# First cross attention of a gated cross-attention block: negative maxima added by TensorE in PSUM, rstd by a GpSimd power

## What is computed

```python
x = x + jnp.tanh(g_xattn[0]) * _L0_xattn_ref(_layernorm(x, axis=-1), ctx_1024, ...)
# inside, 16 sequences, 64 queries and 64 context rows (48 main, 16 "dca"), 16 heads of 16
q = _ln((x @ Wq + bq).reshape(b, s1, H, HD), qn_w, qn_b)
k = _ln(kv[..., :HD], kn_w, kn_b)
k_dca = _ln(kv_dca[:, :, 0], kn_dca_w, kn_dca_b)
ctx = _attn(qT, k..., v...)               # softmax(q k^T / 4) v over the 48 main rows
ctx_dca = _attn(qT, k_dca..., v_dca...)   # the same over the 16 dca rows, its own softmax
return (ctx + DCA_WEIGHT * ctx_dca) @ Wo + bo
# _ln divides by sqrt(var + 1e-6) within each head
```

## Time and profile before

| | |
|---|---|
| median of 3 runs | 534.36 us (534.05 to 830.44) |
| span of the profiled execution, first to last instruction | 530.4 us |
| median less span | 4.0 us |
| phase A in that span | up to about 161 us |
| busy in the span | PE 443.2, DVE 362.0, ACT 199.5, POOL 170.8 us |

### The profile page before, as it was taken

One profiled execution on the slowest core, in us unless ns is written; L12 is line 12 of the kernel. 1 busy time (PEld: TensorE's weight loads), 2 busy tenths in 40 slices (PEclk: granted clock), 3 DMA queues, 4 the chain that ended last, 5 costly groups with the idle time before them and its releaser, 6 DMA issues.

```text
span 530.4 us, 8960 instructions
## 1 busy us (share of the span) xinstructions
PE 443.2 (84%) x2992; PEld 399.9 (75%) x2992; DVE 362.0 (68%) x785; ACT 199.5 (38%) x390; POOL 170.8 (32%) x204
## 2 busy tenths in 40 slices
PE   0575948666468999999998999989999998989996
PEld 0455837555468889898997978968998896888886
DVE  5768688695506557585757698698788779855542
ACT  2355535363221333233233534454344344423331
POOL 3004132232300221212123453564454365333322
PEclk9958886959556999999899969998996998999999
DMA  8111010100200020010201001001000100000000
GB/s 242 30 59 59 1 59 0 60 2 6 93 1 0 1 99 0 15 83 0 99 0 53 1 0 53 1 0 51 0 0 1 50 0 0 0 0 21 20 20 21
DMA packets 6628, 15.96 MB, mean 30 GB/s; under 512 B 1090, under 2 KB 4291, under 8 KB 6100
## 3 DMA queue, kind: packets, MB, share of 16 engines
q1 hardware_dynamic: 6612, 15.75, 9.1%
HBM read 14.70 MB, written 1.05 MB: 30 GB/s over the span
## 4 chain that ended last, share of the span: by engine, by line
PE 51%; issue 17%; DVE 13%; POOL 11%; ACT 4%; DMA 3%; POOLq 0%; DVEq 0%; ACTq 0%; SPq 0%
PE ps L287 34%; DVE work L1277 4%; PE ps L1071 3%; PE ps L468 3%; POOL work L1329 2%; POOL workr L1453 2%; PE ps L803 2%; POOL workA L554 2%; PE ps L458 2%; PE ps L824 2%; PE ps L827 1%; POOL wB_lo L560 1%; PE ps L258 1%; DMA stage<-in_wC 1%; PE ps L1083 1%
## 5 line engine op out<-in xcount | busy, mean ns | idle before, releaser
L287 PE MATMUL ps<-xT_hi,wB_hi 128*128 128x256 f32 x224 | 67.7, 302 | 1.7 <-POOL wB_lo L1334 1.7
L287 PE MATMUL ps<-xT_lo,wB_hi 128*128 128x256 f32 x224 | 64.6, 289 | 0.0
L287 PE MATMUL ps<-xT_hi,wB_lo 128*128 128x256 f32 x224 | 64.4, 288 | 0.0
L287 PE MATMUL ps<-wB_hi,workr 128*128 128x256 f32 (+1 forms) x224 | 52.4, 297 | 3.8 <-POOL workr L1453 3.4
L287 PE MATMUL ps<-wN_hi,shared_r 128*128 128x256 f32 x256 | 52.7, 301 | 0.0
L995 POOL TENSOR_TENSOR workr<-work,workr 128x256 fp32r<-128x256 f32 (+1 forms) x36 | 22.9, 636 | 83.8 <-ACT workr L878 83.8
L287 PEld LDWEIGHTS ps<-xT_hi,wB_hi 128*128 128x128 f32 x224 | 44.1, 197 | 4.0 <-issue 1.9
L1329 POOL TENSOR_SCALAR work<-work,lut_step,lut 128x344 f32<-128x344 int32 (+1 forms) x72 | 46.5, 660 | 1.6 <-POOL wB_lo L1334 1.6
L1277 DVE COPY_PREDICATED work<-work 128x1376 f32<-128x1376 int32 (+5 forms) x36 | 43.6, 1212 | 4.0 <-DVE work L1277 1.1
L287 PEld LDWEIGHTS ps<-wN_hi,shared_r 128*128 128x128 f32 x256 | 43.9, 206 | 1.5 <-DVE shared_r L1240 1.5
L287 PEld LDWEIGHTS ps<-xT_lo,wB_hi 128*128 128x128 f32 x224 | 44.2, 197 | 0.0
(11 more groups left out here) (178 smaller groups left out, 1161.3 us busy)
## 6 DMA issues: line engine op xcount, KB each, us to landing
stage<-in_wC SPq DMA_DIRECT2D x4, 1280.0 KB, 5.4
stage<-in_wB SPq DMA_DIRECT2D x4, 768.0 KB, 4.3
stage<-in_idx SPq DMA_DIRECT2D x4, 536.0 KB, 4.0
stage<-in_wA SPq DMA_DIRECT2D x2, 512.0 KB, 5.6
out<-x SPq DMA_DIRECT2D x4, 256.0 KB, 2.2
x<-in_x SPq DMA_DIRECT2D x1, 768.0 KB, 7.2
ctx_T<-in_ctx_T SPq DMA_DIRECT2D x1, 512.0 KB, 7.6
ctx_n<-in_ctx_n SPq DMA_DIRECT2D x4, 128.0 KB, 2.2
```

The costliest lines, as they stand in the source:

```text
L287: last = nc.tensor.matmul(out, l, r, start=start and i == 0, stop=stop and i == 2)
```

## The change

1. VectorE writes the negated maxima of a tile as float32r (`dve_A_top`) and subtracts nothing. Both tiles' maxima stand at the head of the group.
2. TensorE adds them to the scores in PSUM: per tile four matmuls with the identity (a float32r copy, `ident_A`) as weights and the negated maxima, repeated 48 or 16 times, as the moving operand (`pe_A_shift`). The score matmuls leave their sums open for it. Both shifts stand behind the next group's query matmuls.
3. ScalarE's exponentials read PSUM and write `probs`; both stand before the next group's square.
4. ScalarE's logarithm and exponential of the variance and VectorE's three correcting instructions are gone; GpSimd raises the 128x64 variances to -0.5 (`pool_A_rstd`), behind the first tile's scaling, and in the start between the two layer-norm powers.

```diff
                     k = c * BG + 2 * t + b
                     last = nc.tensor.matmul(o[:, :, b, :], qx[:, k].rearrange("p h n -> p (h n)"),
-                                            kx[:, k], start=True, stop=True)
+                                            kx[:, k], start=b == 0, stop=False,
+                                            skip_group_check=True)
             last.then_inc(*A["scores_done"].up())
+
+        def pe_A_shift(pe, g, t):
+
+            pe.wait_ge(*A["maxed"].at(g, 2 * t + 2))
+            for c in range(2):
+                o = ps[:, 2 * t + c, :].rearrange("p (k n) -> p k n", n=S)
+                for i, (lo, hi) in enumerate(PARTS):
+                    first = 16 * i + 8 * c
+                    last = nc.tensor.matmul(o[:, :, lo:hi], ident_A, bc_last(neg_maxA[:, t, first:first + 8], hi - lo),
+                                            start=False, stop=True, skip_group_check=True)
+            last.then_inc(*A["shifted"].up())
...
-        def act_A_guess(act, n):
-
-            act.wait_ge(*A["grp_var"].at(n, 1))
-            nc.scalar.activation(gln, gvar, ACT.Ln).then_inc(*A["act"].up())
-            act.wait_ge(*A["act"].at(n, 1))
-            nc.scalar.activation(guess, gln, ACT.Exp, scale=-0.5).then_inc(*A["grp_guess"].up())
...
         def dve_A_scale(dve, n):
 
-            dve.wait_ge(*A["grp_guess"].at(n, 1))
-            nc.vector.tensor_tensor(gsq, guess, guess, ALU.mult).then_inc(*A["dve"].up())
-            dve.wait_ge(*A["dve"].at(n, 2))
-            nc.vector.scalar_tensor_tensor(out=gfix, in0=gsq, scalar=-0.5, in1=gvar, op0=ALU.mult,
-                                           op1=ALU.mult).then_inc(*A["dve"].up())
-            dve.wait_ge(*A["dve"].at(n, 3))
-            nc.vector.scalar_tensor_tensor(out=grs, in0=gfix, scalar=1.5, in1=guess, op0=ALU.add,
-                                           op1=ALU.mult).then_inc(*A["dve"].up())
-            dve.wait_ge(*A["dve"].at(n, 4))
+            dve.wait_ge(*A["grp_rstd"].at(n, 1))
             nc.vector.tensor_tensor(heads, heads, bc_last(grs, HD0), ALU.mult).then_inc(*A["scaled"].up())
...
         def act_A_exp(act, g, t):
-            act.wait_ge(*A["shifted"].at(g, 2 * t + 2))
-            v = split_tokens(probs[:, t])
-            nc.scalar.activation(v, v, ACT.Exp, scale=HD0 ** -0.5).then_inc(*A["exp_ready"].up())
+            act.wait_ge(*A["shifted"].at(g, t + 1))
+            nc.scalar.activation(split_tokens(probs[:, t]), split_tokens(ps[:, 2 * t:2 * t + 2, :]), ACT.Exp,
+                                 scale=HD0 ** -0.5).then_inc(*A["exp_ready"].up())
...
-        def dve_A_shift(dve, g, t):
+        def dve_A_top(dve, g, t):
 
             dve.wait_ge(*A["scores_done"].at(g, t + 1))
             s = split_tokens(ps[:, 2 * t:2 * t + 2, :]).rearrange("p (k n) -> p k n", n=S)
             for i, (lo, hi) in enumerate(PARTS):
-                nc.vector.tensor_reduce(mxA[:, t, 16 * i:16 * i + 16], s[:, :, lo:hi], AX,
-                                        ALU.max).then_inc(*A["maxed"].up())
-            for i, (lo, hi) in enumerate(PARTS):
-                dve.wait_ge(*A["maxed"].at(g, 2 * t + i + 1))
-                nc.vector.tensor_tensor(probs[:, t, :, lo:hi], s[:, :, lo:hi],
-                                        bc_last(mxA[:, t, 16 * i:16 * i + 16], hi - lo),
-                                        ALU.subtract).then_inc(*A["shifted"].up())
+                nc.vector.tensor_reduce(neg_maxA[:, t, 16 * i:16 * i + 16], s[:, :, lo:hi], AX,
+                                        ALU.max, negate=True).then_inc(*A["maxed"].up())
...
+            pe.wait_ge(ident_A_ready, 1)
 
         def pe_A(pe, g, more, two_more):
             n = g + 1
             if more:
                 pe_A_q(pe, n)
+            pe_A_shift(pe, g, 0)
+            pe_A_shift(pe, g, 1)
             pe_A_probs(pe, g, 0)
...
@@ -618,16 +617,13 @@
             n = g + 1
             act_A_prep(act, g)
             act_A_exp(act, g, 0)
+            act_A_exp(act, g, 1)
             if more:
                 act_A_square(act, n)
-                act_A_guess(act, n)
-            else:
-                act_A_exp(act, g, 1)
             if two_more:
                 act_A_ctx(act, g + 2)
             act_A_probs(act, g, 0)
             if more:
-                act_A_exp(act, g, 1)
                 act_A_qk(act, n)
                 act_A_k(act, n)
...
-            dve_A_shift(dve, g, 0)
+            dve_A_top(dve, g, 0)
+            dve_A_top(dve, g, 1)
             if more:
                 dve_A_kv(dve, n)
                 dve_A_q(dve, n)
             dve_A_sum(dve, g, 0)
             if more:
                 dve_A_var(dve, n)
-            dve_A_shift(dve, g, 1)
             if more:
                 front_stats(dve, g + 2, (g + 2) % GROUPS)
                 dve_A_scale(dve, n)
...
+        def pool_A_rstd(pool, n):
+
+            pool.wait_ge(*A["grp_var"].at(n, 1))
+            nc.gpsimd.tensor_tensor(grs, gvar, expo[:, 0:1].broadcast_to([P, 64]), ALU.pow
+                                    ).then_inc(*A["grp_rstd"].up())
+
         def pool_A_start(pool):
             front_pool(pool, 0)
+            pool_A_rstd(pool, 0)
             front_pool(pool, 1)
 
         def pool_A(pool, g, more, two_more):
+            n = g + 1
             pool_A_prep(pool, g)
             pool_A_scale(pool, g, 0)
             if more:
+                pool_A_rstd(pool, n)
                 front_pool(pool, g + 2)
             pool_A_scale(pool, g, 1)
```

More of the change, by code:

```diff
@@ L202, in build @@
         front = signals("front", stat=4, var_ready=1, rstd_ready=1, xn_ready=2, xT_done=1, hi_ready=1, lo_ready=1)
-        A = signals("A", dve=4, act=1, ctx_hi=2, ctx_lo=2, kv_done=2, q_done=1, kv_ready=6, q_ready=1,
-                    squared=1, grp_var=1, grp_guess=1, scaled=1, qT_done=2, kT_ready=2 * PAIRS0,
-                    qx_ready=2, scores_done=2, maxed=4, shifted=4, exp_ready=2, summed=4, recip_ready=2,
+        A = signals("A", dve=1, ctx_hi=2, ctx_lo=2, kv_done=2, q_done=1, kv_ready=6, q_ready=1,
+                    squared=1, grp_var=1, grp_rstd=1, scaled=1, qT_done=2, kT_ready=2 * PAIRS0,
+                    qx_ready=2, scores_done=2, maxed=4, shifted=2, exp_ready=2, summed=4, recip_ready=2,
                     probs_ready=4, pT_done=2, pT_ready=2, pv_done=1, an_ready=4, anT_done=1, an_hi=1, an_lo=1,
@@ L209, in build @@
         A_prep_in = sem("A_prep_in")
+        ident_A_ready = sem("ident_A_ready")
         CH = EC + 1
@@ L309, in build @@
         an = take(TILES * D).rearrange("p (t n) -> p t n", t=TILES)
-        gsum, gssq, gvar, gln, guess, gsq, gfix, grs = (take(64) for _ in range(8))
-        mxA, smA, rcA = (take(64).rearrange("p (t n) -> p t n", t=TILES) for _ in range(3))
+        gsum, gssq, gvar, grs = (take(64) for _ in range(4))
+        smA, rcA = (take(64).rearrange("p (t n) -> p t n", t=TILES) for _ in range(2))
         take_r = carver(workAr)
@@ L314, in build @@
         aT_hi, aT_lo = (take_r(DC * TG).rearrange("p (c n) -> p c n", c=DC) for _ in range(2))
+        neg_maxA = take_r(TILES * 32).rearrange("p (t n) -> p t n", t=TILES)
+        ident_A = take_r(P)
         def ctx_rows(g, lo, hi):
@@ L605, in act_A_start @@
             act_A_square(act, 0)
-            act_A_guess(act, 0)
+            act.wait_ge(const_in, 16)
+            nc.scalar.copy(ident_A, ident).then_inc(ident_A_ready, 1)
             front_upper(act, 1, 7)
```

2 lines of the change are left out of this document (1 added, 1 removed).

## The result

The changed kernel takes 569.81 us (median of 4 runs, 563.26 to 575.58) against 534.25 before: a ratio of 1.0587, 95% interval [1.0544, 1.063], so slower by some 6%.

What follows compares the result with a forecast made beforehand. Two almost level paths to TensorE's turn bound cross attention. Start +0.9, group 0 +1.1, waits -0.6 and group 3 -0.2 make +1.2 us; span 531.6 plus 4.0 gives 535.6 us, range 526 to 559.

Steps and rivals of the forecast that it cites:

- the power is long: Rival, GpSimd's queue between the two scalings: from X = 3.6 each us costs four; X = 8 gives 554 us; chance 0.27.
- the likeliest case: Power at 2.8 us, clock as before, shift at 0.52 us a tile: 535.6 us, the case alone spanning 532 to 545.
- X: Duration of GpSimd's 128x64 power to -0.5, in the start and groups 0 to 2: 2.8 us, bounds 0.83 and 20.2.
- 4X - 12.4: Change of the whole time in us once X exceeds 3.6, from the start and three groups; passes 2% at X = 5.8.
- start, X - 1.87: Head scaling in the start, queued behind the power: -0.7 us up to X = 1.15, X - 1.87 beyond, +0.9 at 2.8.
- groups 1 and 2, X - 3.6 - 0.2 each: Power free up to X = 3.6, one us per us beyond; the 0.2 us wait for GpSimd's second scaling is gained.
- group 0, the same, with the shift +1.1: Shift queued behind 12 key/value and 12 query matmuls, so the first tile's sums start later: +1.1 us.
- second path: VectorE's head scaling and second tile's sums, then GpSimd's second scaling: ends at 13.1 + X, T counted from the group's start.
- The first path: First tile's sums (T = 4.32), scaling, transposes, values and next group's turn, until T = 16.70; the change does not move it.
- The shift at full rate: TensorE's four shift matmuls per tile at 0.51 ns a column: 0.52 us, plus about 0.2 until ScalarE sees it.
- The rival of a float32 price: Shift matmuls on TensorE run as plain float32, 2.96 us a tile: 542.8 us, still within 2%; chance 0.06.
- Kept clock: Rival: shifts break TensorE's idle time, so it keeps full clock: 519.6 us, group 3 alone about 528; chance 0.09.

Runs made afterwards that it cites:

- power only: The kernel before with only GpSimd's 128x64 power in place of ScalarE's guess and VectorE's correction: 568.2 us, ratio 1.0639.
- long filling: The changed kernel with 30 unused identity transposes where TensorE waits for the scaled heads and 22 where it waits for the second scaling: 561.81 us, ratio 1.0534.
- shift only: The changed kernel without the power, ScalarE's guess and VectorE's correction put back in their old places: 533.81 us, ratio 1.0011.
- half-width run: The changed kernel with the power on 32 of the 64 columns, the others left at 1: 551.31 us, ratio 1.0342.
- old order: "shift only" with the kernel before's order in all three queues: 529.1 us, 0.9932; with 30 identity transposes ahead of the first tile's: 526.06 us, 0.9892.
- filled kernel before: The kernel before with 34 unused identity transposes after the query matmuls of each group: 539.96 us, ratio 1.0117.

## Why the prediction was wrong

I forecast 535.6 us, range 526 to 559, and gave "slower by over 2%" 0.27. Measured: 569.8, outside the range. The power makes the loss, as the rival "the power is long" has it; the likeliest case had the size of the power wrong.

**The step that failed is the term X**, the price of the 128x64 power, "the weakest number here". I had bounds of 0.83 and 20.2 us from rows, and both held: it is 10.52. My value of 2.8 came from an assumption that no row carried, that a power costs fifteen multiplies of 2.26 ns a column. It costs 0.158 us a column, 70 multiplies. Of the 0.63 us by which the two-column power exceeds a multiply's fixed part, half was in fact the columns' share (2 x 0.158). The upper bound, "all of it grows with the columns", was off by a factor of 2, my value by nearly 4. The figure for branches in the Trainium skill (GPSIMD Engine Reference, Performance versus the Vector engine), by which X was estimated at 1.3, was further off than mine: the trace has 10.52.

**The waits of the formula that turns X into time held; the clock was missing from it.** The rival "the power is long" gave 4X - 12.4, 2% from X = 5.8. With X = 10.52 that is +29.7, or 564.0 us; the two runs behind the ratio took 563.26 and 566.58, and 1.0587 times 534.25 is 565.6. How near that is owes something to luck, since the formula has no term for the clock behind the waits and even the groups of one execution differ in it. Its parts, read in "power only" and in the changed kernel with the long filling, where the clock was full behind the waits:

| term | forecast at X = 10.52 | power only | long filling |
|---|---|---|---|
| start, X - 1.87 | +8.65 | +8.2 | +8.1 |
| groups 1 and 2, X - 3.6 - 0.2 each | +6.7 | +7.3, +7.0 | +6.2, +6.0 |
| group 0, the same, with the shift +1.1 | +6.7 or +7.8 | +10.3, of it 3.4 half clock | +7.6 |

In the changed kernel itself the second path reads as forecast: the second scaling at T = 112.77 + 2.11 - 91.26 = 23.6, forecast 13.1 + X = 23.6.

**The first path.** "The first path does not move" was right: the sums of group 1 start at T = 95.58 - 91.26 = 4.32, forecast 4.32, and "shift only" measures 1.0011.

**The shift at full rate.** Right: four matmuls took 0.76 us with their pipeline, 0.52 plus 0.2 forecast. The rival of a float32 price (2.96) falls. With "shift only" group 0 is 0.6 us longer (1.1 forecast) and groups 1 and 2 are 0.3 and 0.4 us shorter (0.2 forecast). The row of 5.91 us behind the rival's price was not wholly at half clock (0.50 up to 37 us, 0.72 and 1.00 after it), so that price was a little low; nothing hangs on it.

**Kept clock.** Right to expect that it would not come: values 3.67 or 3.65 in the first tile of groups 0 to 2. But the prediction asked of the clock only whether it would be kept. It did not ask what the new waits would do to it. Behind the 1.80 us ahead of the second transposes the values and scores ran at half clock in all three groups of the half-width run, and the formula lacks that: some 3 to 4 us a group there. With this term left out, 4 x 5.42 - 12.4 gives 543.6 us, where "half width" measured 551.3.

**The range.** Its upper end stood at X = 9.2, not because a row spoke against more, but because I had given the long power little chance. With bounds 24 times apart and the value between them a guess, the slower side deserved about half of the chance, and the range had to reach to X near 11 or beyond.

## What to carry to other kernels

An operation whose price per column no row shows must not be priced as a multiple of a cheap one. With only a tiny instance at hand, give a good share of the chance to the case that all it takes beyond the fixed part grows with the columns; here that was too high by a factor of 2, and would still have put the loss on the right side. Before an edit moves work into another engine's queue, work out the size from which the queue becomes the path (here 3.6 us), since that threshold could be read from the rows of before while the size itself could not. And when a part of a change gains nothing, look at the order it came with: the shift without subtraction became a gain (0.9932) when each queue kept its old order, so that the first tile's sums started 1.1 us earlier.

## What the runs showed of the hardware that was not expected

- A GpSimd power costs 0.158 us a column of 128 partitions between 2 and 64 columns (16 columns, once, took 4.51 us and are off that line), and 64 columns cost the same whether the exponent is one repeated column or a tile; a multiplication of the same 128x64 takes 0.29 us against 10.52.
- A wait of TensorE of only 0.66 us (filled kernel before) or 1.80 us (half width) ahead of the second tile's transposes left the granted clock at half for the values and scores behind it, about 7 us of work that otherwise takes 4. But the same 1.80 us in "power only" did so in group 0 and not in groups 1 and 2, and with the old order waits of 1.70 and 1.96 us left the clock full (values 2.00 and 1.97). The length of the wait alone does not decide; what does stays open.
- Float32 transposes of the identity, used as filling, bring the granted clock up by themselves: in group 1 of the long filling it rose from 0.50 to 1.00 while TensorE ran nothing else. Eight transposes behind a filling mostly took 1.09 us against 1.97, though not always (1.36 and 1.69 in one group each).
- Matmuls with a float32r moving operand that is repeated 48 or 16 times showed no cost for the repetition: 1,024 columns in 0.76 us, the last one's drain included.
